# Causal attention with the q, k and v products split into float32r parts

## What is computed

```python
h = _rms(x, n1_w)
heads = lambda w_: (h @ w_.T).reshape(B, T, HEADS, HD).transpose(0, 2, 1, 3)
q = _rms(heads(wq), qn_w)
k = _rms(heads(wk), kn_w)
v = heads(wv)
scores = jnp.einsum('bhqd,bhkd->bhqk', q, k) * HD ** (-0.5)
scores = jnp.where(causal[None, None], scores, -jnp.inf)
attn = jax.nn.softmax(scores, axis=-1)
ao = jnp.einsum('bhqk,bhkd->bhqd', attn, v) ... @ wo.T
x = x + ao
```

## Time and profile before

| | us |
|---|---|
| Median of 3 runs | 4516.61 |
| Lowest and highest | 4506.92, 4517.59 |
| The profiled execution | 4504.19 |
| Its span, first to last instruction | 4502.3 |

### The profile page before, as it was taken

One profiled execution on the slowest core, in us unless ns is written; L12 is line 12 of the kernel. 1 busy time (PEld: TensorE's weight loads), 2 busy tenths in 40 slices (PEclk: granted clock), 3 DMA queues, 4 the chain that ended last, 5 costly groups with the idle time before them and its releaser, 6 DMA issues. The chain is left out here.

```text
span 4502.3 us, 85912 instructions
## 1 busy us (share of the span) xinstructions
PE 3970.4 (88%) x29034; PEld 2739.8 (61%) x29034; DVE 2662.7 (59%) x6134; ACT 2006.3 (45%) x3548; POOL 993.3 (22%) x1840
## 2 busy tenths in 40 slices
PE   5999999645558999999979999999899999999999
PEld 3555555334445555555535555555588888888888
DVE  5766666578765777777746666666643333333333
ACT  2555555376653555555535445545432222223222
POOL 2443434000002333333224344444210000000000
PEclk8999999877777999999979999999999999999999
DMA  3000000000000000000000000000120000000000
GB/s 94 12 12 9 12 10 9 25 1 0 0 11 10 10 9 9 9 12 9 3 9 15 19 19 19 19 19 14 45 71 15 29 14 28 14 28 14 24 18 15
DMA packets 79354, 80.32 MB, mean 18 GB/s; under 512 B 4880, under 2 KB 76560, under 8 KB 79248
## 3 DMA queue, kind: packets, MB, share of 16 engines
q1 hardware_dynamic: 79248, 78.91, 5.6%
HBM read 53.73 MB, written 25.17 MB: 18 GB/s over the span
## 5 line engine op out<-in xcount | busy, mean ns | idle before, releaser
L621 DVE TENSOR_REDUCE a_neg_max<-psum 128x2 f32<-128x512 f32 x512 | 328.9, 685 | 192.6 <-PE psum L791 191.3
L1293 DVE TENSOR_REDUCE d_neg_max<-psum 128x2 f32<-128x256 f32 (+1 forms) x512 | 261.3, 553 | 280.6 <-PE psum L1456 278.6
L621 DVE TENSOR_REDUCE c_neg_max<-psum 128x2 f32<-128x512 f32 x512 | 328.6, 684 | 130.4 <-PE psum L791 129.7
L521 ACT ACTIVATE c_exps<-psum 128x512 f32<-128x512 f32 x512 | 277.9, 594 | 243.7 <-PE psum L813 243.6
L521 ACT ACTIVATE a_exps<-psum 128x512 f32<-128x512 f32 x512 | 278.0, 594 | 205.6 <-PE psum L813 205.2
L1196 ACT ACTIVATE d_exps<-psum 128x512 f32<-128x512 f32 (+1 forms) x512 | 223.3, 488 | 285.7 <-PE psum L1483 285.7
L2408 PE MATMUL psum<-e_hidden_l,e_e_l_high 128*128 128x512 f32 x1024 | 321.0, 395 | 0.8 <-POOL e_e_l_low L2170 0.8
L810 PE MATMUL psum<-a_q_by_parity,a_k_stationary 32*128 32x512 f32 x1536 | 270.9, 432 | 23.2 <-ACT a_exps L521 22.5
L791 PE MATMUL psum<-c_k_by_parity,c_q_high_low 32*128 32x512 f32 x1536 | 286.6, 440 | 5.2 <-DVE c_neg_max L621 5.2
L791 PE MATMUL psum<-a_k_by_parity,a_q_high_low 32*128 32x512 f32 x1536 | 267.9, 437 | 9.7 <-DVE a_neg_max L621 9.5
L810 PE MATMUL psum<-c_q_by_parity,c_k_stationary 32*128 32x512 f32 x1536 | 262.7, 436 | 3.8 <-ACT c_exps L521 3.0
(11 more groups left out here) (386 smaller groups left out, 9934.9 us busy)
## 6 DMA issues: line engine op xcount, KB each, us to landing
x_all<-in_x_dram SPq DMA_DIRECT2D x4, 2048.0 KB, 16.0
a_ctx<-in_ctx_t_dram SPq DMA_DIRECT2D x32, 256.0 KB, 2.7
c_ctx<-in_ctx_t_dram SPq DMA_DIRECT2D x32, 256.0 KB, 2.7
x_rows<-d_x SPq DMA_DIRECT2D x32, 256.0 KB, 2.2
out_dram<-d_y SPq DMA_DIRECT2D x32, 256.0 KB, 2.3
e_x<-x_rows SPq DMA_DIRECT2D x16, 512.0 KB, 4.3
e_y<-out_dram SPq DMA_DIRECT2D x16, 512.0 KB, 4.1
out_dram<-e_y SPq DMA_DIRECT2D x16, 512.0 KB, 3.2
```

Of the source, the lines that this page charges most:

```text
L521: s_.activation(EX[:, t], st_bank[t % 3], ACT.Exp).then_inc(exp_done, 1)
L621: v.tensor_reduce(NM[:, :, t, r, m], sc_bank[u % 3].rearrange("p (e k) -> p e k", e=2), AX.X, ALU.max, negate=True).then_inc(sc_used, 1)
L1293: v.tensor_reduce(NM[:, :, t, r, m], sc_bank[u % 3][:, 0:512 if t else 256].rearrange("p (e k) -> p e k", e=2), AX.X, ALU.max, negate=True ...
```

## The change

The rows `XNT` and the scaled weights `Wq` become pairs of a high and a low part, `XNS` and `WH`, both `float32r`. Lines 1431 and 1435 make three products in place of one, as `PARTS` names them. ACT's copy of p0 now writes the high part (it signals `xh_ready`, and frees the bank no more). A new item `p0` on DVE, `rows_low`, stands in its order after NM0 and ahead of s8: it waits for ACT's copy, subtracts the high part from what is in PSUM, writes the low part, and frees the bank. In the prologue it stands between R1 and N. The raw weights are loaded into the space of the exponentials (`EX`); DVE makes high and low parts of them as the stage starts, and PE and ACT wait for five steps in place of three.

```diff
-MHA_DVE = "s0 s1 R0 s2 s3 T0- s4 s5 R1 s6 s7 NM0 s8 s9 T1- N s10 s11 PX- s12 s13 s14 s15 NM1 PR-"
+MHA_DVE = "s0 s1 R0 s2 s3 T0- s4 s5 R1 s6 s7 NM0 p0 s8 s9 T1- N s10 s11 PX- s12 s13 s14 s15 NM1 PR-"
...
-            Wq = sb("wqkv", [P, DC, 3 * D])
+            WH = sb("wqkv_high_low", [P, 2, DC, 3 * D], F32R)
-            XNT = sb("xnt", [P, DC, S])
+            XNS = sb("xnt_high_low", [P, 2, DC, S], F32R)
+            WRAW = EX[:, 0:DC]
...
-                act.wait_ge(w_scaled, 3)
+                act.wait_ge(w_scaled, 5)
...
-                        s_.activation(XNT[:], w.rearrange("p (m s) -> p m s", m=2), ACT.Copy).then_inc(free[f], 1)
+                        s_.activation(XNS[:, 0], w.rearrange("p (m s) -> p m s", m=2), ACT.Copy).then_inc(xh_ready, 1)
...
-                    v.tensor_scalar(Wq[:, cc], Wq[:, cc], PB[:, 2 + cc:3 + cc], None, ALU.mult).then_inc(w_scaled, 1)
+                    v.tensor_scalar(WH[:, 0, cc], WRAW[:, cc], PB[:, 2 + cc:3 + cc], None, ALU.mult).then_inc(w_scaled, 1)
                 v.tensor_scalar(PB[:, 0:1], PB[:, 0:1], DK ** -0.5, None, ALU.mult).then_inc(w_scaled, 1)
                 dve.wait_ge(w_scaled, 3)
+                for cc in range(DC):
+                    v.scalar_tensor_tensor(WH[:, 1, cc], WRAW[:, cc], PB[:, 2 + cc:3 + cc], WH[:, 0, cc].bitcast(F32),
+                                           ALU.mult, ALU.subtract).then_inc(w_scaled, 1)
+                dve.wait_ge(w_scaled, 5)
+
+                def rows_low(s):
+                    b = at(s, 3)[0]
+                    dve.wait_ge(xh_ready, b + 1)
+                    f = place(s, "p0")[0]
+                    v.tensor_tensor(XNS[:, 1], w_bank[f].rearrange("p (m s) -> p m s", m=2), XNS[:, 0].bitcast(F32), ALU.subtract).then_inc(free[f], 1)
...
                     elif k in (1, 2):
                         for cc in range(DC):
-                            i = mm(w[:, :], XNT[:, cc, (k - 1) * P:k * P], Wq[:, cc, 0:2 * D], start=cc == 0, stop=cc == DC - 1)
+                            for q, (x, y) in enumerate(PARTS):
+                                i = mm(w[:, :], XNS[:, x, cc, (k - 1) * P:k * P], WH[:, y, cc, 0:2 * D],
+                                       start=cc == 0 and q == 0, stop=cc == DC - 1 and q == 2)
                     elif k == 3:
                         for t in range(2):
                             for cc in range(DC):
-                                i = mm(w[:, t * S:(t + 1) * S], XNT[:, cc, t * P:(t + 1) * P], Wq[:, cc, 2 * D:3 * D], start=cc == 0, stop=cc == DC - 1)
+                                for q, (x, y) in enumerate(PARTS):
+                                    i = mm(w[:, t * S:(t + 1) * S], XNS[:, x, cc, t * P:(t + 1) * P], WH[:, y, cc, 2 * D:3 * D],
+                                           start=cc == 0 and q == 0, stop=cc == DC - 1 and q == 2)
```

More of the change, by code:

```diff
@@ L946, in mha @@
             w_in, w_scaled, consts = sem("weights_in"), sem("w_scaled"), sem("consts")
-            xn_ready = sem("xn_ready")
+            xn_ready, xh_ready = sem("xn_ready"), sem("xnt_high")
             full = [sem(f"work_full{k}") for k in range(2)]
@@ L1041, in _ @@
                 for n in range(3):
-                    sp.dma_start(Wq[:, :, n * D:(n + 1) * D],
+                    sp.dma_start(WRAW[:, :, n * D:(n + 1) * D],
                                  a[f"D_w{'qkv'[n]}"].rearrange("(c p) e -> p c e", p=P)).then_inc(w_in, 16)
@@ L1356, in item @@
                         row_max(s, int(x[1:]))
+                    elif x == "p0":
+                        rows_low(s)
                     elif x == "N":
@@ L1374, in prologue @@
                     for i in (-3, -2, -1):
-                        for x in ("R0", "R1", "N"):
+                        for x in ("R0", "R1", "p0", "N"):
                             item(x, started(i))
@@ L1395, in _ @@
                 mm, tr = nc.tensor.matmul, nc.tensor.transpose
-                pe.wait_ge(w_scaled, 3)
+                pe.wait_ge(w_scaled, 5)
                 def use(s, x):
```

## The result

| | before | after |
|---|---|---|
| Median, 20 runs each, on the same chips | 4510.19 | 4519.95 |
| The profiled execution | 4504.19 | 4519.68 |
| Its span | 4502.3 | 4517.6 |

The ratio is 1.0021, 95% interval 1.0011 to 1.0031: slower by 0.2%, 9.5 us. The forecast was +2.5 on the profiled execution and 4519 in all.

The account below looks back on a forecast made before the run. A period was taken as PE from p4 to s4, then DVE from s4 to T1-. -.66 - .13 + .60 = -.19, times 29 is -5.5 us; once only 0, clock +8: +2.5, 4519 beside the median, range 4497 to 4541.

Parts of the forecast that it names:

- p1 and p2: Products of q and k on PE: six float32r matmuls each, 1.39 us, together saving .66 us a period.
- p3: Product of v on PE: 1.5 us, beside DVE's chain, so only the .13 us that s6 waits comes back.
- The subtraction: New DVE instruction between NM0 and s8: 680 ns, adds .60 us to DVE's part; its added wait costs nothing.
- Once only: Ahead of the loop: +2.0 us for the weights' low parts, set against -2.2 in the first three batches: zero.
- The clock: PE's wait before p4 grows from 1.5 to about 2.2 us: 5 more falls to half speed, 16 in all, +8 us.
- Rival 1: The clock falls to half speed behind the wait before p4 in every period: +20 us, 4537; chance .14.
- Rival 2: The v product on PE gets slower, 2.5 us, as load and product add up: 4535 to 4551 us; chance .09.
- Rival 3: DVE's chain has .6 us of unseen slack, so all of PE's saving is paid: -23 us, 4494; chance .12.

Follow-up runs that it names:

- v_plain: The kernel after with only the v product back to one plain float32 product, low parts left out of v; a single run, 4546.3 us.
- pool_later: The kernel after with POOL's products for the first half waiting until DVE is done with NM0; ratio to before .9997.
- dve_alone: The kernel before with only the new DVE subtraction between NM0 and s8, its result unused, products still plain float32; median 4564.9 us, ratio to before 1.0106.
- low_after_t1: The kernel after with the DVE subtraction moved behind T1-; median 4485.6 us, ratio to before .9943.

## Why the prediction came out as it did

The time was right to 1 us on the median of 4519.95, and by the ratio to before the difference was +9.5, not +2.5. That the level fits so well is luck: the forecast starts from a median of three runs of before (4516.61), 6.4 us above that of 20 (4510.19), and the change was forecast 7 us too small. What the forecast had right is the signs: a shorter period and more falls of the clock. The terms came out unequally.

- **p1 and p2: right.** .61 to .63 against .66. Six instructions take 1.48 and not 1.39, but the first begins up to .08 us sooner behind the transposes.
- **p3: the size right, the step wrong.** 1.53 against 1.5. "Only the .13 that s6 waits comes back" is the step that failed: .30 came back. .14 at s6, as forecast; and .16 in NM0, which ends with POOL's products, which begin behind PE's x3 and so behind p3 (v_plain and pool_later). The prediction had seen that "the instructions of NM0 wait for each other", allowed up to .13 for it and took none. It had not looked at what ran on POOL meanwhile. That is why a period got .31 shorter and not .19.
- **The subtraction: right.** .69 us between NM0 and s8, .57 on the path by itself, .59 after the products are in. Its wait for ACT cost nothing.
- **Once only:** +1.4 against 0.
- **The clock: the sign and the count right, the price wrong.** The wait was 2.1 (2.2 forecast), the falls 17 (16). But the 18 us are more than twice the 8 of the sum: 6 of the falls were long ones at 3.1 us, and every fall had been priced at 1.6. That falls go in proportion to the wait was an estimate and isn't shown: at 1.5 us there were 11, 8 and 3 of 27, at 1.8 there were 12, at 2.1 there were 17, 20, 25 and 25. What stands, with one profiled execution of each, is that the short waits of .4 to .7 had none, and that the kernels with 2.1 had more than all with less. What else sets the count is open.
- The two errors have opposite signs: -.12 x 28 = -3.4 from p3, +10 from the clock. With +1.4 once only, that makes up the 8 between the forecast of +2.5 and the +10.7 that the stage lost; the other 5.1 of the span lie ahead of the stage, whose start moves by more than that between runs.
- **Rival 1** (a fall in every period) did not come in this kernel, but its mechanism is real: dve_alone and v_plain fell in 25 of 27. A chance of .14 was not too high.
- **Rival 2** (256 columns don't cover their loads) is wrong: twelve instructions, each with a load of 128 by 128 weights of its own, start .12 us apart (only the second .22 behind the first). So the rule of the Trainium skill ("TensorE: Matmul & The Clock Gate", Part 3, "The mechanism"), that a load overlaps only where the row group differs, is not borne out for 256 columns either; the same section also lets a load go ahead into a background weight buffer, and no run here shows whether these do. With 12 x .107 for the loads and 12 x .10 or more for the products it would be 2.5 us, an estimate from that page's "LDWEIGHTS", and more by the .19 us that the profile gives each of these loads; 1.53 was measured. The prediction also had that rule cheaper than it is for p1 and p2: six loads and six products come to 6 x (.107 + .21) = 1.9 us, an estimate from the same page, .2 more than before and not .1 less.
- **Rival 3** (the subtraction hides) is wrong in this place, by dve_alone, and right one place further on, by low_after_t1.

## What to carry to other kernels

An instruction added where another engine waits for the ones behind it can cost more than its length, since the idle time that it makes can lower the clock (dve_alone: 28 x .57 = 16 us of length and 25 of clock); move it behind the last instruction that someone waits for (some 35 us of after's time, by the ratios). Price a longer wait with the clock's loss in it, and where a wait can't be shortened, try filling it with matmuls that nobody reads (15 and 30 us here). And before saving is called hidden behind another engine's chain, look at every engine that ran beside the chain's slow instructions, POOL's included.

## What the hardware did that was not expected

- **DVE instructions that end with POOL's.** A cast of 128x16 takes .20 us alone and up to .49 beside POOL's products of 128x512; it ends .06 to .10 us after them. The subtraction of 128x16 behind it takes .19 us alone and .47 to .50 beside POOL's cast of 128x512, and ends .04 us after that one. pool_later shows that POOL is the cause; through what the two meet was not tried.
- **Long falls.** Half speed for 6.8 us in place of 3.4, in 6 of after's 17. In every kernel they were seen only where the fall began .9 us or later after p4; the reason is open.
- **Falls that repeat themselves.** In dve_alone 20 falls in a row began .25 to .84 us after p4, each within .09 us of the one in front, and the periods were 30.6 to 30.8 long. In such a chain nearly every period falls, which a law of proportion can't give.
